# Two pairs side by side before the values, the row pieces dealt out anew, and another order at the end

## What is computed

```python
q, k, v = x @ Wq.T + bq, x @ Wk.T + bk, x @ Wv.T + bv
a = q @ k.T / sqrt(512) + adj + adj
x = layernorm(x + softmax(a) @ v)

feats = einsum('nf,hfd->hnd', x, W)                    # 8 heads of 64
dense = leaky_relu(e_self[:, :, None] + e_neigh[:, None, :])
dense = dense + -1e10 * (1.0 - adj)
out = relu(concat(softmax(dense) @ feats) + b)
x = layernorm(x + out)
```

## Time and profile before

| what | value |
|---|---|
| median of 3 runs | 1766.46 us (1763.76 to 1771.32) |
| profiled execution | 1767.35 us, span 1765.5 us |
| TensorE matmul busy | 1579.3 us, 89% |
| VectorE busy | 1232.4 us, 70% |
| GpSimd busy | 863.9 us, 49% |
| ScalarE busy | 540.7 us, 31% |
| granted TensorE clock, mean | 0.968 |
| transfers | 395 MB, 224 GB/s over the span |

### The profile page before, as it was taken

The page is one execution under the profiler, slowest core; times in us unless marked ns, Lnnn a source line. Parts: engine busy times, 40 slices in busy tenths (PEclk is TensorE's granted clock), DMA queues, the critical chain, the costliest instruction groups (busy, mean ns, idle before and its releaser), DMA issues.

```text
span 1765.5 us, 27937 instructions
## 1 busy us (share of the span) xinstructions
PE 1579.3 (89%) x10052; PEld 963.4 (55%) x10052; DVE 1232.4 (70%) x2465; ACT 540.7 (31%) x805; POOL 863.9 (49%) x821
## 2 busy tenths in 40 slices
PE   7989688999999989999999899999999899999720
PEld 3434266666666656666666566666565566644300
DVE  5888666668875877578758786788577867753144
ACT  4546300122233223322322223222322232245335
POOL 2966400355554545355535544454454445569452
PEclk9999899999999999999999999999999999999965
DMA  7366675568765876577667865786577757646356
GB/s 256 137 237 229 249 257 179 193 208 279 255 209 184 275 266 215 186 271 287 224 187 267 292 216 167 260 317 221 174 265 253 240 171 243 212 144 205 111 165 247
DMA packets 188316, 395.11 MB, mean 224 GB/s; under 512 B 20624, under 2 KB 26768, under 8 KB 187024
## 3 DMA queue, kind: packets, MB, share of 16 engines
q1 hardware_dynamic: 183056, 376.52, 63.2%
q0 software_dynamic: 5120, 16.78, 2.8%
HBM read 335.55 MB, written 57.67 MB: 223 GB/s over the span
## 4 chain that ended last, share of the span: by engine, by line
PE 67%; DVE 13%; DMA 10%; issue 4%; SPq 3%; POOL 1%; ACT 1%; another core or an unknown queue 0%; DVEq 0%; ACTq 0%; POOLq 0%
PE O L729 28%; PE S L701 28%; DMA big<-in_adj 6%; PE X L658 4%; PE O L658 3%; PE S L658 3%; DVE cand L1169 2%; DVE ring L1205 1%; DMA yb<-y_scratch 1%; DVE big L1054 1%; DVE work L1228 1%; PE X L770 1%; DVE ring L1405 1%; DVE xr L1254 1%; DVE vring L1089 1%
## 5 line engine op out<-in xcount | busy, mean ns | idle before, releaser
L729 PE MATMUL O<-vring,ring 128*128 128x512 f16 x3072 | 740.2, 380 | 3.2 <-POOL ring L617 2.5
L701 PE MATMUL S<-yb,big 128*128 128x256 f16 x5376 | 672.7, 274 | 69.1 <-DVE ring L1205 55.3
L701 PEld LDWEIGHTS S<-yb,big 128*128 128x128 f16 x5376 | 514.8, 98 | 248.5 <-DVE ring L1205 56.8
L617 POOL TENSOR_TENSOR ring<-work,ring 128x512 f16<-128x512 f32 x256 | 306.2, 1196 | 666.1 <-ACT ring L888 666.1
L729 PEld LDWEIGHTS O<-vring,ring 128*128 128x128 f16 x3072 | 300.4, 98 | 277.5 <-issue 5.8
L998 ACT ACTIVATE work<-ring 128x512 f32<-128x512 f32 x256 | 160.8, 628 | 819.9 <-DVE ring L1196 763.5
L1205 DVE TENSOR_TENSOR ring<-S,ring 128x256 f32<-128x256 f32 x512 | 214.7, 419 | 231.4 <-PE S L701 230.0
L625 POOL TENSOR_TENSOR work<-work 128x512 f32<-128x512 f32 x248 | 338.1, 1363 | 0.0
L1210 DVE TENSOR_TENSOR ring<-S,ring 128x256 f32<-128x256 f32 x384 | 162.3, 423 | 74.8 <-PE S L701 56.3
L1228 DVE TENSOR_TENSOR work<-work,ring 128x512 f32<-128x512 f32 x248 | 202.8, 818 | 0.1
L1169 DVE MAX8 cand<-big 128x8 f32<-128x512 f32 x256 | 171.0, 684 | 32.5 <-DMA big<-in_adj 32.3
(11 more groups left out here) (129 smaller groups left out, 914.8 us busy)
## 6 DMA issues: line engine op xcount, KB each, us to landing
ring<-in_adjT SPq DMA_DIRECT2D x256, 256.0 KB
big<-x_scratch SPq DMA_DIRECT2D x128, 512.0 KB
vring<-v_scratch SPq DMA_DIRECT2D x256, 256.0 KB
big<-in_adj SPq DMA_DIRECT2D x256, 256.0 KB, 5.6
yb<-y_scratch SPq DMA_DIRECT2D x56, 256.0 KB
y_scratch<-yb SPq DMA_DIRECT2D x7, 1792.0 KB, 9.3
ring<-in_xT SPq DMA_DIRECT2D x8, 1024.0 KB, 7.1
v_scratch<-vring SPq DMA_DIRECT2D x32, 256.0 KB, 2.5
```

Source lines behind the costliest of these rows:

```text
L617: pool.tensor_tensor(ring16[:, e % SLOTS, 1, :], pf[:, e % NPF, :], ring16[:, e % SLOTS, 0, :], ALU.subtract).then_inc(lo_done, 1)
L701: mm = pe.matmul(bank, keys_of(p, keys, a, c), yb[:, b % 2, queries, m, c, :], start=(start and c + a + m == 0), stop=(c == 1 and a == 1), ...
L729: mm = pe.matmul(O[j][:, :], ring16[:, e % SLOTS, a, j * P:(j + 1) * P], vring[:, e % NV, m, :], start=(k + a + m == 0), stop=(k == NT - 1 ...
```

## The change

- Steps 0 to 17 are done two pairs at a time: product n of the first pair, of the second, then n + 1. The second pair uses the first halves of banks O[0] and O[1], which are free before the values. There are four buffers for key pairs up to pair 17 (the fourth lies where the pieces come later), adjacency tiles for two pairs are loaded together, `maximum` runs two pairs behind.
- The last query block's splits (`queries_lo`, `query_sums_lo`) move on VectorE behind the first and the fourth reads of pairs 0 and 1; the store of its y moves to step 4, the loads of block 1's parts of y from steps 0 to 6 to steps 6 to 12.
- Pieces: 1 or 3 a step without scaling up to step 127, then 2 a step up to step 139. The first piece of a step is loaded ahead of the key pair, and what follows its scan (`scanned`) stands behind the read of the fourth chain product.
- From chunk 222 on VectorE makes the lo half (`last_lo`) in place of GpSimd.
- The last 12 chunks' values are done by group: all 12 into O[0], then O[1], O[2], O[3], with the row tiles between; their value tiles are loaded into free slots of `ring`. The last tiles of odd number have halves and transposes of their own (in `pf`), so that a tile doesn't wait for the one before. The proof moves into the loop of the last chunks, and TensorE's matmul for it ahead of group 0.
- The last normalisation has nine groups, the last two of two tiles; three groups go by squares; the reciprocal root is four operations, for two groups together where possible; VectorE writes the last tile.

```diff
+        last_h, last_T = pf[:, 0, :].bitcast(F16), pf[:, 1, :].bitcast(F16)
+
+        def halves(t):
+            return last_h.rearrange("p (a n) -> p a n", a=2) if t >= NT - JB and t % 2 else x1h
+
+        def transposed(t):
+            return last_T.rearrange("p (a c n) -> p a c n", a=2, c=KC) if t >= NT - JB and t % 2 else x1T
...
+        NE = NB + 1
+        GROUPS = [range(e * JB, (e + 1) * JB) for e in range(NB - 1)] + [range(NT - JB, NT - 2), range(NT - 2, NT)]
+        BY_SQUARES = (1, 3, 5)
+        TOGETHER = ((0, 1), (2, 3), (4, 5), (6,), (7,), (8,))
...
-            return 0 if not LAG <= s < NCP - 2 else 1 if 2 <= s % NP <= 8 else 3
+            if LAG <= s < NCP:
+                return 1 if 2 <= s % NP <= 8 else 3
+            return 2 if NCP <= s < NCP + 12 else 0
 
         def pieces_at(s):
-            total = sum(piece_load(i) for i in range(STEPS))
             before = sum(piece_load(i) for i in range(s))
-            return range(before * NT * NPC // total, (before + piece_load(s)) * NT * NPC // total)
+            return range(before, before + piece_load(s))
...
+        def banks(p):
+            return (O[0][:, 0:QH], O[1][:, 0:QH]) if p < LAG and p % 2 else (S[0][:, 0:QH], S[1][:, 0:QH])
...
+        def buffer_of(p):
+            return p % (NX + 1) if p < LAG else p % NX
...
+        LO_FIRST = 2 * (NCP - LAG + 1)
+        TAIL = 12
+        PV_ALL = NC - TAIL + 1
+
+        def values_of(e):
+
+            return vring[:, e % NV] if e < NC - TAIL else ring16[:, (e - 2 * LAG + TAIL) % SLOTS]
...
+                if held_before(p) is not None:
+                    sp.wait_ge(chain_done, chain_count(held_before(p), 3))
...
+            load_pair(3)
...
+                if s < LAG:
+                    for c in range(min(2 * s + 4, SLOTS), min(2 * s + 6, SLOTS)):
+                        load_adj(c)
+                elif 2 * s + 3 < NC:
+                    load_adj(2 * s + 3)
+                if s == LAG - 1:
+                    sp.wait_ge(chain_done, chain_count(NP - 1, 3))
+                for p in pieces_at(s + 1)[:1]:
+                    load_piece(p)
+                if s + NX + 1 < LAG:
+                    load_pair(s + NX + 1)
+                elif LAG <= s + NX < NCP:
                     load_pair(s + NX)
                 load_chunks(1)
-                for p in pieces_at(s + 1):
+                if s >= LAG and 2 * s + 4 < NC:
...
+                if s == 4:
+                    store_y(NB - 1)
+                if s == 6:
+                    sp.wait_ge(y_out[1], 16 * (NB // 2))
+                if 6 <= s < 13:
+                    load_y_part(1, s - 6)
...
+                        if e < LO_FIRST:
+                            pool.wait_ge(hi_done, e + 1)
+                            pool.tensor_tensor(ring16[:, e % SLOTS, 1, :], pf[:, e % NPF, :], ring16[:, e % SLOTS, 0, :],
+                                               ALU.subtract).then_inc(lo_done, 1)
+                        else:
+                            pool.wait_ge(exp_done, e + 1)
...
+                    if p == 1:
+                        pe.wait_ge(y_copied, NB * KC)
+                    before = p - 2 if p <= LAG else p - 1
+                    if before >= 0:
+                        pe.wait_ge(chain_read, chain_count(before, 3))
...
+            for s in range(0, LAG, 2):
+                for n in range(4):
+                    for p in (s, s + 1):
+                        chain_product(p, n)
+                        if n < 3:
+                            side_product(p, n)
+                    if n == 1 and s == NP:
+                        transpose_maxima(0)
+                    if n == 3 and s == NP:
+                        broadcast_maxima(0)
+            for s in range(LAG, STEPS - TAIL // 2):
...
+            pe.wait_ge(ok_chain, 9)
+            pe.wait_ge(chain_read, 4 * NCP)
+            pe.matmul(S[0][0:1, 0:1], okw[:, 0:1], ones[:, 0:1], start=True, stop=True).then_inc(sums_ready, 1)
+
+
+            J0, J1, J2, J3 = range(NT - JB, NT)
+            for e in range(NC - TAIL, NC):
+                values(e, 0)
+            row_sums(NB - 1)
+            for e in range(NC - TAIL, NC):
+                values(e, 1)
             pe.wait_ge(flag_set, 1)
-            transpose_x1(first)
-            for j in range(JB):
-                if j + 1 < JB:
-                    transpose_x1(first + j + 1)
-                feats(first + j)
+            transpose_x1(J0)
+            for e in range(NC - TAIL, NC):
+                values(e, 2)
+            feats(J0)
+            transpose_x1(J1)
+            for e in range(NC - TAIL, NC):
+                values(e, 3)
+            feats(J1)
+            transpose_x1(J2)
+            feats(J2)
+            transpose_x1(J3)
+            feats(J3)
...
-            queries_lo(NB - 1)
-            query_sums_lo(NB - 1)
...
+            def last_lo(e):
+                dve.wait_ge(hi_done, e + 1)
+                dve.tensor_tensor(ring16[:, e % SLOTS, 1, :], pf[:, e % NPF, :], ring16[:, e % SLOTS, 0, :],
+                                  ALU.subtract).then_inc(lo_last, 1)
...
+            for s in range(0, LAG, 2):
+                for n in range(4):
+                    for p in (s, s + 1):
+                        reads(p, n)
+                    if s == NP and n == 0:
+                        for c in range(NT - 4, NT):
+                            maximum(c)
+                    elif 0 < s < NP:
+                        maximum(2 * s - 4 + n)
+                    if s == NP and n == 2:
+                        maxima(0)
+                    if s == 0 and n == 0:
+                        queries_lo(NB - 1)
+                    if s == 0 and n == 3:
+                        query_sums_lo(NB - 1)
+            subtract(0)
+            subtract(1)
+            maximum(NT)
+            maximum(NT + 1)
...
-                scans(pieces[:1])
+                for p in pieces[:1]:
+                    scan(p)
                 if scoring:
-                    read_chain(s, 3, 1, 0)
+                    reads(s, 3)
                 if turning is not None:
                     evict(turning, 2)
                     evict(turning, 3)
-                scans(pieces[1:])
+                for p in pieces[:1]:
+                    scanned(p)
...
+            for e in range(2 * (STEPS - TAIL // 2 - LAG + 1), NC):
+                last_lo(e - 1)
+                subtract(e)
+                if e == NC - 4:
                     find(NT - 1)
-                if s == NCP + 3:
...
+            last_lo(NC - 1)
```

454 lines of the change are left out of this document (255 added, 199 removed).

## The result

The changed kernel took 1741.6 us (median of 4 executions, 1737.9 to 1742.3) against 1767.1 for the kernel before beside it: a ratio of 0.985, with a 95% interval of 0.9825 to 0.9876. I had forecast 1721. The profiled execution took 1742.32 us, its span is 1740.5, so 25.0 us went from the span where I had summed 46.7.

What follows compares the result with a forecast made beforehand. It took TensorE as the bound in the middle, with 52 us of loss there to waits. Parts -18.7 - 33 + 5 + 14 - 14 = -46.7 us from 1767.35 gave 1721; range 1690 to 1752, own range 1703 to 1740.

Steps and rivals of the forecast that it cites:

- rival 3: Steps before the values: double steps are held by the transfers, +18 us, time 1739; chance 12%.
- Rival 4: Splits wait for GpSimd everywhere: 24 splits in steps 128 to 139 0.7 us longer, block 3 more, time 1740; 8%.
- part 5: Last normalisation, first gather to end: 59 us instead of 72.7, -14 us, bounds -19 and -6.
- part 2: Pieces of rows in the middle: never more than three a step, earlier issue, finds behind TensorE's read; -33 us of 52.
- Part 1: Stretch before the values, two pairs side by side: -11 - 13.3 + 5.6 = -18.7 us.
- Part 4: Last 12 chunks: period 3.1 us, TensorE idle some 25, first gather 78 us after step 139; +14 us.
- part 3: Steps 128 to 139: 88 us against 83.4, VectorE nearly full with some 75 us of work; +5 us.
- the start: Up to pair 2: it starts in effect at about 221.6 instead of 232.6, gain 11 us.
- The double steps: Before the values: 9.8 us each against 11.7, seven times, gain 13.3; 0.3 us for the second pair's adjacency tiles.
- The store: Last y's store of 1.8 MB at step 4, ahead of adjacency tiles: loss 5.6 us, bounds 0 and 6.7.
- t0: The end of step 139, from which part 4 counts; first gather forecast at t0 + 78.
- Rival 5: Slower than before: last chunks' serial splits eat all gains from 7.8 us a period, 1780 at 9 us; chance 3%.

Runs made afterwards that it cites:

- d_adj: Changed kernel with a double step's four adjacency tiles asked for together, ahead of the next two pairs of keys; ratio 0.9759 to the kernel before.
- f_pieces: Kernel before with only the weights of the row pieces unscaled, so that no step has four pieces; ratio 0.9764 to the kernel before.
- g_order: Changed kernel with the first piece's earlier load and the finds behind TensorE's read undone, never four pieces kept; ratio 0.9872 to the kernel before.
- after_again: Changed kernel run once more, nothing edited; ratio 0.9846 to the kernel before.
- h_hold: Changed kernel with SyncE holding every store of the output until the last gather has landed; ratio 0.9871 to the kernel before.
- k_best0: Changed kernel with j_tail0's edits, d_adj's load order and output groups normalised one by one; 1686.1 us, ratio 0.9587 to the kernel before.
- a_swap: Changed kernel with chunk e's subtraction issued before chunk e-1's split in VectorE's last loop; ratio 0.9799 to the kernel before.
- c_parts: Changed kernel with the last y stored in seven parts at steps 1 to 7, not one store at step 4; ratio 0.9824 to the kernel before.
- j_tail0: Changed kernel with the deferral undone, f_pieces' weights, proof and last find after step 128, row-tile transposes one ahead; 1711.8 us, ratio 0.9670 to the kernel before.

## Why the prediction was right, and where not

**Direction and range** held: the time fell by more than 9 us, 1741.6 lies in 1690 to 1752. But the gain was 25.5 us where I had 46, and 1741.6 lies 1.6 us outside the narrower range of my own forecast (1703 to 1740). It is close to what rivals 3 and 4 gave (1739, 1740), by chance: neither mechanism is in the profile at the size that they had. By the spans the sum missed by 21.6 us; part by part it was too low by 7.9, too high by 5.0, too low by 4.3, too high by 0.7 and, in part 5, too low by 15.1. So the 5 us of part 2 hid some of the rest. The mechanisms of parts 1, 2 and 4 are in the profile, with sizes that were off in the first two; part 3 had its wait wrong in part, and part 5 failed.

**Part 1, the start** came as worked out: pair 2 at 220.75, I had 221.6. **The double steps** were mis-sized: I had 0.3 us for the second pair's adjacency tiles and the six double steps beside that of the store were 0.4 to 1.7 us longer than 9.8, 6.1 us in all. d_adj shows it by taking it away: 9.63 to 9.77 without, my 9.8 was right for a kernel whose tiles are there. I had written that these tiles go out behind 512 KB of keys and are wanted 2.4 us later, with a landing of 6.6 us in the rows as rival 3's case; the size stood in my own text, and I took the small end. **The store** cost 8.6 us (18.4 - 9.8) where I had 5.6: the wait of 5.5 is right, but 3 us more came, with the granted clock at 0.66 from 250 to 260 us. I hadn't priced the clock behind a stop of TensorE in this place, only at the end.

**Part 2** was right in its mechanism and 5 us small. Its three causes are not alike: f_pieces and g_order show that never four is nearly all of it, and the earlier issue and the finds behind the read are 1 us together. I said 25 four-piece steps, there were 26.

**Part 3** was mis-sized: +9.3, I had +5. TensorE waits for VectorE's splits five times, 9.5 us in all, of which 4.96 at 1525.33. VectorE's 75 us of work were right (72.2), but it isn't full: it waits itself. Four times it waits for ScalarE's half of a row tile, 12.3 us in all, and the split that TensorE needs stands behind that. I had counted VectorE's work and not its order. The transfers weren't the bound that I had set beside it: they moved 261 GB/s at a share of 0.77, TensorE waited 1.2 us for a value tile, and the 336 GB/s that I took for "all there is" is no limit, for d_adj moved 353 at a share of 0.94 and after_again 404 at 1.03.

**Part 4** was right: t0 + 77.2 where I had 78, the period 3.15 (3.1), TensorE idle 24.2 (25). Behind it the first group ran at half clock, as taken. I had set the lock of the Trainium skill's page "SBUF — State Buffer", section "SBUF: two separate sides", against the shortest row. The 34 splits of the profile after:

```profile
L1399 DVE TENSOR_TENSOR ring<-work,ring x34: 674/1196/1771, 1499.8 to 1622.7; 128x512 f16<-128x512 f32 x34
```

The 14 that start while GpSimd runs no sum take 0.67 to 0.69 us. The 20 that start while a sum (L708) runs take what is left of the sum and 0.55 us more: 16 of them 1.16 to 1.22 with 0.61 to 0.67 left, four 1.77 with 1.22 left. The trace agrees with the page: such a split does its work when the sum has ended, and the wait is counted as its busy time. I had the rule on one side and the shortest row on the other, periods of 3.4 and 2.7; it is 3.15. From split to subtraction VectorE takes 1.12 us in the loop and 0.61 at 1613.69, where no sum runs, so, as an estimate from these two, about 0.5 us of each period of 3.15 are this wait. No run takes the sum away. Rival 4 had this mechanism: in steps 128 to 139 it added 8.0 us to the 23 splits together, where the rival had 0.7 on each of 24; the four of 1.77 are those that TensorE waits for.

**Part 5, the last normalisation, is the step that failed**: I had -14 and it is +1.1. I took the old end, with its unnamed wait, as the price of the old order, put the last group at +49 by the time when gathers land, and gave it 10 us from its start, because it had fewer tiles and operations. In the profile after the last group starts 58.6 us after the first gather, 9.6 later than I had, and the end comes 15.3 us behind that, 5.3 more. The undisturbed runs show what holds it. Without the wait the old order takes 64.6 us and the new 65.5 to 67.1. The last group starts in the new one at +52.6 (1719.61 in after_again) and needs 14.5 us from there: stores and gathers fill the queues from 1700 to 1715 (347 and 404 GB/s) and VectorE waits 6.34 us for a gather, until 1710.03; with the stores held (h_hold) it waits 1.95 and the last group starts at +48.5. Behind that wait VectorE is busy 10.6 of 11 us. ScalarE has eight tiles of a pair ahead of the last groups' roots, its last normalisation ends at +60.5, and the last store lands 5.3 us after its issue. So fewer operations save nothing ahead of that wait, and what comes after it is longer than the 10 us that I gave it. With the groups one by one (k_best0, 63.8) the new order is 0.8 us ahead of the old one. My lower bound of this part (-6) was wrong too: I had no case in which the new order doesn't gain.

Of the rivals, rival 3 was nearest for the double steps (I gave 18 us, it was 6.1 beside the store), but by order, not by capacity. Rival 5's loop is what the profile shows, at the 3.15 us that I had, far from the 7.8 from which it would have decided.

## What to carry to other kernels

Before forming anything side by side, look at what the queue of loads brings between the two: here one changed line in the order of SyncE's list was worth 15 us, more than the 10.8 us by which the whole change had brought the values forward, and a store of 1.8 MB did no harm once the tiles stood ahead of it. Where N items share B buffers, see that no step gets B + 1 of them: one weight table was worth more than the whole change. Work handed to an engine for a deferred stage must be pipelined there as it was before: subtract ahead of split took 10 of the 28 us off that the deferral cost, and even the best deferral tried only broke even. When an engine takes on work that another waits for, look at what it waits for itself ahead of that work. And a stage's time in one profile can hold waits that another execution doesn't have, so take it twice before counting it as gain.

## What the runs showed of the hardware

On VectorE, in the stretch where the 32 gathers and the first stores go out, instructions that wait for an earlier one of the same engine stood idle 1.23 us each for this, and 3.3 to 7.6 us once, in five of the profiles: 1.4 us from start to start in the profile after, where the same instructions take 0.2 in after_again. They go with profiles in which hundreds of landings are missing, cost some 7 to 9 us, whatever the kernel, and began ahead of the first store in the profile after (1697.6, store at 1700.23). Their cause stays open: h_hold ran at a time without them.

A subtraction of two SBUF tensors on VectorE that starts while GpSimd runs a sum of two (1.27 us) ends 0.55 us behind that sum, in 20 of 20 cases of the profile after, and takes 0.67 to 0.69 us in the 14 without a running sum. In a_swap, where VectorE has no gap, GpSimd's sums grow to 1.47.

TensorE's 12 matmuls took 2.74 us in place of 1.47 right behind a wait of 5.5 us (after) and one of 3.2 us (c_parts), the lower of its two levels (1.2 GHz); behind the wait of 1.52 us at 268.33 in c_parts they took 1.48. The length of the stop doesn't decide it alone, for behind 3.13 us in j_tail0 they took 1.48:

```profile
286.17 1.48 PE L783 MATMUL O<-yb,big 128*128 128x256 f16 x12 [3.13 <-DVE ring L1321]
```

With the stop taken away (d_adj), the granted clock stays 1.00 from 230 to 300 us.

A tile issued 0.5 us behind a store of 1.8 MB on the same queue landed 10.0 us after its issue, 0.6 us after the store (after_again). Seven small stores in a row of loads cost nearly what one large cost (seven double steps in 80.9 us and in 82.6 to 87.1), and one large behind the loads that the next double step needs cost nothing (68.2).
